# A factorisation-machine tower on one core: first tile gathered in two passes of 64 samples, the second pass transposed inside the first tile's steps

## The reference

```python
e = jnp.stack([tbl_0[ids[:, 0]], ..., tbl_32[ids[:, 32]]], axis=1)        # (1024, 33, 128)
row, col = np.triu_indices(33, k=1)
inner = x[:, row] * x[:, col]                                            # (1024, 528, 128)
fm = relu(einsum('bpd,ad->bpa', inner, attn_W) + attn_b)
scores = einsum('ba,bpa->bp', gnn_feature, fm)
attn = softmax(scores, axis=1)
attn_output = einsum('bp,bpd->bd', attn, inner) * 100.0
h = concatenate([gnn_feature, attn_output, gnn_feature], axis=1)
h = relu(h @ W_top1 + b_top1); h = relu(h @ W_top2 + b_top2); y = h @ W_top3
```

## Time and profile before

| what | value |
|---|---|
| median of 3 runs | 1306.75 us |
| the profiled execution, its own time | 1305.15 us |
| its span, first to last instruction | 1303.1 us |
| granted TensorE clock, mean | 1.000 |
| TensorE busy | 1219.5 us (94%) |
| VectorE busy | 1160.7 us (89%) |
| ScalarE busy | 1066.3 us (82%) |
| GpSimd busy | 479.5 us (37%) |
| DMA, mean over the span | 45 GB/s |

### The profile page before, as it was taken

The page is one execution under the profiler, slowest core; times in us unless marked ns, Lnnn a source line. Parts: engine busy times, 40 slices in busy tenths (PEclk is TensorE's granted clock), DMA queues, the critical chain, the costliest instruction groups (busy, mean ns, idle before and its releaser), DMA issues.

```text
span 1303.1 us, 22956 instructions
## 1 busy us (share of the span) xinstructions
PE 1219.5 (94%) x9486; PEld 951.5 (73%) x9486; DVE 1160.7 (89%) x643; ACT 1066.3 (82%) x1166; POOL 479.5 (37%) x271
## 2 busy tenths in 40 slices
PE   1499999999999999999999999999999999999997
PEld 1377777777777877778777777777777787777776
DVE  2499899997999989998999989999899988999964
ACT  2488999789887998879987799878988799877872
POOL 6586784018800486006840088102880000000000
DMA  3212310311113111130102111031111300012000
GB/s 105 99 34 85 64 30 25 108 37 29 33 27 109 31 28 27 29 114 25 32 24 86 58 31 31 15 112 38 29 31 29 104 17 1 1 44 59 13 1 1
DMA packets 54294, 58.58 MB, mean 45 GB/s; under 512 B 10536, under 2 KB 48560, under 8 KB 53168
## 3 DMA queue, kind: packets, MB, share of 16 engines
q1 hardware_dynamic: 45728, 39.81, 10.2%
q0 software_dynamic: 8448, 17.32, 5.0%
q10 hardware_dynamic: 16, 0.00, 0.0%
HBM read 36.12 MB, written 17.31 MB: 41 GB/s over the span
## 4 chain that ended last, share of the span: by engine, by line
PE 69%; ACT 18%; issue 9%; POOL 2%; DVE 1%; DMA 0%; ACTq 0%; POOLq 0%
PE scores L551 19%; PE ring L522 13%; PE ring L529 11%; PE ring L531 9%; PE ring L530 9%; ACT inner_hi L284 8%; ACT fm L276 8%; PE ring L579 4%; POOL x_rows L252 2%; PE ring L561 2%; PE ring L596 1%; PE scores L607 1%; ACT exp_pairs L292 1%; ACT attn L300 1%; DVE inner L391 1%
## 5 line engine op out<-in xcount | busy, mean ns | idle before, releaser
L276 ACT ACTIVATE fm<-ring,attn_b_sb 128x704 f32<-128x704 f32 x768 | 621.8, 867 | 165.6 <-PE ring L522 95.5
L391 DVE TENSOR_TENSOR inner<-xt 128x2112 f32<-128x2112 f32 x256 | 602.3, 2353 | 90.0 <-PE ring L531 37.8
L252 POOL DMA_INDIRECT x_rows<-in_tbl,ids_all x264 | 477.0, 1807 | 496.6 <-PE ring L561 407.0
L398 DVE TENSOR_TENSOR inner_lo<-inner,inner_hi 128x1760 fp32r<-128x1760 f32 (+2 forms) x256 | 473.5, 1850 | 18.1 <-ACT inner_hi L284 17.9
L529 PE MATMUL ring<-inner_hi,attn_wt_lo 128*128 128x352 f32 x1185 | 452.4, 382 | 20.3 <-ACT fm L276 17.3
L284 ACT CAST inner_hi<-inner 128x1760 fp32r<-128x1760 f32 (+2 forms) x256 | 401.0, 1567 | 5.4 <-DVE inner L391 5.4
L530 PE MATMUL ring<-inner_lo,attn_wt_hi 128*128 128x352 f32 x1185 | 382.4, 323 | 0.0
L531 PE MATMUL ring<-inner_hi,attn_wt_hi 128*128 128x352 f32 x1185 | 382.2, 323 | 0.0
L529 PEld LDWEIGHTS ring<-inner_hi,attn_wt_lo 128*128 128x128 f32 x1185 | 222.8, 188 | 79.6 <-ACT fm L276 54.8
L522 PE MATMUL ring<-inner,attn_wt 128*128 128x352 f32 x702 | 265.8, 482 | 12.5 <-ACT fm L276 8.0
L551 PE MATMUL scores<-fm,gnn_blocks 128*32 128x264 f32 x4096 | 254.4, 389 | 3.9 <-ACT exp_pairs L292 3.0
(11 more groups left out here) (50 smaller groups left out, 268.5 us busy)
## 6 DMA issues: line engine op xcount, KB each, us to landing
x_dram<-x_rows SPq DMA_DIRECT2D x8, 2112.0 KB, 6.7
x_fields<-x_dram SPq DMA_DIRECT2D x120, 128.0 KB, 3.0
x_rows<-in_tbl,ids_all POOLq DMA_INDIRECT x264, 3.5
attn_t<-attn_turned SPq DMA_DIRECT2D x112, 32.0 KB, 1.9
w_sb<-in_W_top SPq DMA_DIRECT2D x2, 512.0 KB, 6.3
x_rows<-x_dram SPq DMA_DIRECT2D x8, 128.0 KB, 3.9
x_fields<-in_r_gnn_feature SPq DMA_DIRECT2D x1, 512.0 KB, 4.1
h<-in_W_top SPq DMA_DIRECT2D x1, 256.0 KB, 6.2
```

The source lines that it names most:

```text
L252: nc.gpsimd.indirect_dma_start(out=x_rows[:, f, :], out_offset=None, in_=tables[f], in_offset=bass.IndirectOffsetOnAxis(ap=ids_all[:, t, f ...
L276: nc.scalar.activation(dst, slot(("hidden", S, j))[:, :, 0:CHUNK], ACT.Relu, bias=attn_b_sb[:, 0:1]).then_inc(s_fm, 1)
L391: nc.vector.tensor_tensor(dst, a, b, ALU.mult).then_inc(s_inner, 1)
L398: nc.vector.tensor_tensor(inner_lo[:, S % LO_BUFS, 0:n * CHUNK], inner[:, S % INNER_BUFS, NATIVE[S] * CHUNK:], inner_hi[:, S % HI_BUFS, 0: ...
```

## The change

Tile 0 alone is gathered in two passes. The first 33 indirect DMAs fetch samples 0 to 63 (`EARLY`), the next 33 samples 64 to 127, with indices of their own, `ids_late`, which a second small DMA loads into partitions 0 to 63. TensorE transposes the early rows ahead of step 0 (64 columns instead of 128), ScalarE copies half as much. The late rows are transposed behind steps 8, 9, 10, 11 and 11 (`LATE_AT`), all 128 rows of a field by 128, of which ScalarE copies the upper 64 samples. The product of step 16 (sample 64) waits for them. Tile 1's gathers now wait for the late chunks and for the store of tile 0, which waits for both passes. The steps of the transposes of tile 1 (`XT_AT`) and all later tiles are as before.

```diff
+    EARLY = P // 2
+    LATE_AT = (8, 9, 10, 11, 11)
...
-        jobs = []
+        jobs = [("late", 0, c) for c in range(XJ) if t == 0 and s == LATE_AT[c]]
...
-    units = [("x_t", 0, c) for c in range(XJ)]
+    units = [("early", 0, c) for c in range(XJ)]
...
+        def xt_jobs(kind, t):
+            return {"early": 0, "late": XJ}.get(kind, XJ * (t + 1))
...
             def store_rows(t):
                 for c in range(XJ):
+                    if t == 0:
+                        sp.wait_ge(s_early[c], 16 * fields_in(c))
                     sp.wait_ge(s_gather[c], 16 * fields_in(c) * (t + 1))
...
             sp.dma_start(ids_all[:], ids.rearrange("(t p) f -> p t f", p=P)).then_inc(s_ids, 16)
+            sp.dma_start(ids_late[:], ids[EARLY:P, :]).then_inc(s_ids, 16)
...
                     if t > 0:
-                        pool.wait_ge(s_xt_done, XJ * (t - 1) + c + 1)
+                        pool.wait_ge(s_xt_done, XJ * t + c + 1)
                         pool.wait_ge(s_store, 16 * t)
...
-            pool.wait_ge(s_ids, 16)
-            for t in range(T):
+            pool.wait_ge(s_ids, 32)
+            for f in range(F):
+                nc.gpsimd.indirect_dma_start(
+                    out=x_rows[0:EARLY, f, :], out_offset=None, in_=tables[f],
+                    in_offset=bass.IndirectOffsetOnAxis(ap=ids_all[0:EARLY, 0, f:f + 1], axis=0),
+                ).then_inc(s_early[f // FU], 16)
+            for f in range(F):
+                nc.gpsimd.indirect_dma_start(
+                    out=x_rows[EARLY:P, f, :], out_offset=None, in_=tables[f],
+                    in_offset=bass.IndirectOffsetOnAxis(ap=ids_late[:, f:f + 1], axis=0),
+                ).then_inc(s_gather[f // FU], 16)
+            for t in range(1, T):
                 gather(t)
...
+                own = samples_of(kind)
+                src = slot((kind, t, c))[:, 0:h, 0:min(n, 4) * P].rearrange("p h (f b) -> p (h f) b", b=P)[:, :, own]
+                dst = xt[:, t % 2, own, FU * c:FU * c + n].rearrange("d b f -> d f b")
...
+                    if GROUPS * (S + 3) == EARLY:
+                        dve.wait_ge(s_xt_out, 2 * XJ)
+                        dve.wait_ge(s_repeat, 2 * (K // FU))
...
+            def transpose_x(kind, t, c):
+                signal, loads = (s_early[c], 1) if kind == "early" else (s_gather[c], t + 1)
+                pe.wait_ge(signal, 16 * fields_in(c) * loads)
...
+                rows = EARLY if kind == "early" else P
                 for n in range(fields_in(c)):
-                    last = nc.tensor.transpose(to[:, n // 4, n % 4 * P:(n % 4 + 1) * P], x_rows[:, FU * c + n, :], ident[:])
+                    last = nc.tensor.transpose(to[:, n // 4, n % 4 * P:n % 4 * P + rows], x_rows[0:rows, FU * c + n, :],
+                                               ident[0:rows, 0:rows])
```

More of the change, by code:

```diff
@@ L82, in afm_tower @@
         ids_all = sb("ids_all", [P, T, F], I32)
+        ids_late = sb("ids_late", [P - EARLY, F], I32)
         x_rows = sb("x_rows", [P, F, D])
@@ L131, in afm_tower @@
         s_gather = [sem(f"rows_gathered{c}") for c in range(XJ)]
+        s_early = [sem(f"early_rows_gathered{c}") for c in range(XJ)]
         s_store = sem("rows_stored")
@@ L177, in taken_out, with samples_of @@
                 return s_mlp_out, 3 * a + b + 1
-            return s_xt_out, XJ * a + b + 1
+            return s_xt_out, xt_jobs(kind, a) + b + 1
+        def xt_jobs(kind, t):
+            return {"early": 0, "late": XJ}.get(kind, XJ * (t + 1))
+        def samples_of(kind):
+            return {"early": slice(0, EARLY), "late": slice(EARLY, P)}.get(kind, slice(0, P))
         def fields_in(c):
@@ L300, in scale_attn, with repeat, evacuate_xt @@
                 nc.scalar.activation(attn[:], src, ACT.Copy, scale=inv_sum[:, 0:1]).then_inc(s_attn, 1)
-            def repeat(t, c):
-                act.wait_ge(s_xt_out, XJ * t + c + 1)
-                x = xt[:, t % 2]
+            def repeat(kind, t, c):
+                act.wait_ge(s_xt_out, xt_jobs(kind, t) + c + 1)
+                x = xt[:, t % 2, samples_of(kind)]
                 nc.scalar.copy(x[:, :, F + FU * c:F + FU * c + FU], x[:, :, FU * c:FU * c + FU]).then_inc(s_repeat, 1)
-            def evacuate_xt(t, c):
-                act.wait_ge(s_xt_done, XJ * t + c + 1)
+            def evacuate_xt(kind, t, c):
+                act.wait_ge(s_xt_done, xt_jobs(kind, t) + c + 1)
                 if t > 1:
@@ L337, in _ @@
             for c in range(XJ):
-                evacuate_xt(0, c)
+                evacuate_xt("early", 0, c)
                 if c < K // FU:
-                    repeat(0, c)
+                    repeat("early", 0, c)
             round_inner(0)
@@ L354, in _ @@
                 for kind, of, c in jobs_of(S):
-                    if kind == "x_t":
-                        evacuate_xt(of, c)
+                    if kind in ("x_t", "late"):
+                        evacuate_xt(kind, of, c)
+                    if kind == "late" and c < K // FU:
+                        repeat(kind, of, c)
                     if kind == "mlp":
@@ L359, in _ @@
                 if t + 1 < T and s - 1 in XT_AT[0:K // FU]:
-                    repeat(t + 1, XT_AT.index(s - 1))
+                    repeat("x_t", t + 1, XT_AT.index(s - 1))
             exps(T - 1)
@@ L617, in _ @@
             for c in range(XJ):
-                transpose_x(0, c)
+                transpose_x("early", 0, c)
             pe.wait_ge(s_zero, 3)
@@ L624, in _ @@
                         fields(of, c)
-                    if kind == "x_t":
-                        transpose_x(of, c)
+                    if kind in ("x_t", "late"):
+                        transpose_x(kind, of, c)
                     if kind == "mlp":
```

14 lines of the change are left out of this document (5 added, 9 removed).

## The result

| | median, us | runs |
|---|---|---|
| before | 1306.45 | 4 (1304.79 to 1306.79) |
| after | 1325.20 | 4 (1323.39 to 1328.22) |

The ratio is 1.015 (95% interval 1.0138 to 1.0163): the change makes the kernel 18.8 us slower. The forecast was 1318 us, 11 to 12 us slower, with a range of 1304 to 1330. The profiled execution after took 1325.23 us, its span is 1323.5 us (before 1303.1), its mean granted clock 0.992.

The account below looks back on a forecast made before the run. The pitch of GpSimd's gathers was taken to set the first 50 us, TensorE, VectorE and ScalarE being near-equally busy after. Terms -8.7 + 4.5 + 4.5 + 11 + 1 = +12.3 gave about 1319, stated as 1318 us, range 1304 to 1330.

Parts of the forecast that it names:

- rival A: The forecast itself: slower by 12 us (6 to 18 over g of 0.55 to 0.8); chance 0.60.
- g: Time in us of one 64-row gather on GpSimd: taken as 0.70, between 0.47 and 0.94.
- rival B: A gather of 64 rows costs what one of 128 does: +22 us, 1329; chance 0.15.
- The start: Before the first product: smaller early gathers, transposes and copies gain 8.7 us (1.0 to 16.1).
- One gather per VectorE instruction: Beside the steps GpSimd does one gather per VectorE instruction, two per step, whatever a gather costs by itself.
- Rival C: Late pass not held to one gather per VectorE instruction, 1.0 us a gather: faster, 1302.5 us; chance 0.12.
- Late transposes and copies: Steps 8 to 11 of tile 0: 33 more transposes and copies in halves cost 4.5 us (2.8 to 5.6).
- Step 11: TensorE idles 5.8 us for late chunk 3; with extra gathers in VectorE's gaps, cost 4.5 us (1 to 7).
- Tile 1: Its gathers start at 119.0, behind late pass and store; TensorE waits sum to 12.9, cost 11 us (7 to 14).
- The clock: Slow TensorE weight loads after the longer waits: 0 to 2.5 us for each of two, 1 us in all.

Follow-up runs that it names:

- e3: Kernel before, with 30 measuring gathers of 16 to 128 rows ahead of tile 0's, VectorE idle or beside its products and reductions: 1363.97 us.
- e7: Changed kernel with the products of steps 2 to 27 of tile 0 each in two instructions of 1056 elements: 1307.33 us, ratio 1.001.
- e9: Kernel before with the products of steps 2 to 27 of tile 0 each in two instructions of 1056 elements: 1309.05 us, ratio 1.0003.
- e1: Changed kernel with tile 1's transposes behind steps 19, 22, 26, 28 and 28 of tile 0: 1348.71 us, with the stop of ScalarE at the start.
- e2: Changed kernel, but tile 0 gathered in one pass of 128 rows, transposes and copies still in halves: 1311.96 us, ratio 1.0025 to the kernel before.
- e5: The changed kernel once more, word for word, on another group's chip: 1325.34 us, ratio 1.0144 to the kernel before.
- e8: Changed kernel with 12 and 16 useless TensorE matmuls in the waits of 6.09 and 7.60 us: 1327.17 us, ratio 1.0159 to the kernel before.
- e12: Changed kernel, tile 1's transposes at steps 20, 23, 26, 28, 28 and 12 useless matmuls in step 11; same kernel as e10, another chip: 1319.99 us.
- e10: Changed kernel, tile 1's transposes at steps 20, 23, 26, 28, 28 and 12 useless matmuls in step 11: 1352.33 us, with the stop of ScalarE.
- e11: e7 with tile 1's chunks 3 and 4 transposed one step later each (steps 18, 20, 22, 25, 27): 1350.82 us, with the stop of ScalarE.

## Why the prediction was right, and what was mis-sized

The direction, the place and the mechanism were right. The size was not: the loss is 18.8 us, and rival A, the forecast, had 6 to 18 with g between 0.55 and 0.8. Measured are g = 0.90 and 1325.2, which lies nearer to rival B's 1329 than to 1318. The time stands in the range because that was wide enough to hold most of B. The 7 us between forecast and median (8.1 between the forecast's sum of 12.3 and the 20.4 of the profiled spans) come from the start, and from the clock, whose error is partly hidden by one of the other sign in tile 1's waits.

- **The start: forecast -8.7, measured -3.0 to -3.2.** The mis-sized term is g, "I take the middle, 0.70". It is 0.90 in the changed kernel, 0.91 in e3, near the upper bound of 0.94. The formula held within 0.9 us: 19.4 + 32 x 0.90 = 48.2, measured 47.30. This is 5.5 to 5.7 us of the miss. Rival B had this cost nearly right, and by its sentence (the Trainium skill, page "DMA: Bandwidth & Descriptors", section "Anatomy of one DMA — SWDGE (gpsimd) path": many descriptors can be emitted before their number is felt) the runs agree: in e3 128 rows cost 0.09 us more than 16. Its total of 1329 overshot by 4 us: it gave the start a gain of 1.0 us, where there were 3.0, while its costs of 23.5 us in sum agree with the 23.4 of the rows; the rest is that the medians differ by 18.8 us and the profiled spans by 20.4.
- **One gather per VectorE instruction: right**, with two amendments. e3 has it at 2.26 us a gather beside two-input products and no hold-up beside one-input reductions; e7 turns it into time, 18 us for a third instruction end per step, with e9 as control. And e9 shows that an end is worth a gather only if the gather is ready for it: 128 rows miss the third end that 64 rows catch. Rival C is refuted (the late gathers come at 1.98 us, not 1.0), and with it, for indirect DMAs, the inference in the Trainium skill, page "SBUF — State Buffer", section "Who interferes with whom", that the preparation of DMAs isn't held up.
- **Late transposes and copies: forecast 4.5, measured 5.0** up to the reduction of step 12, in e1 and in e2 alike (5.6 and 5.2 up to the end), inside the bounds of 2.8 to 5.6.
- **Step 11: computed 5.8, taken 4.5, a wait of 6.09 measured.** It cost 7.3 us beyond the late work, of which some 3 are the clock. The further gathers in VectorE's gaps, for which I took 1.3 us off, did not shorten it.
- **Tile 1: forecast 11, measured 10.5, and that agreement is luck.** The 10.5 hold 2.7 us of slow clock, which had a term of its own. The waits themselves were forecast at 12.9 us and are 9.07: 3.3, 5.8 and 3.8 forecast, 1.47, 7.60 and none measured (1.39 for the fourth in e5). The first gather was forecast at 119.0 and came at 119.48. The slow TensorE behind step 11 and each wait let gathers slip in, which I had counted only inside the waits.
- **The clock: forecast 1 in all, 5 to 6 in the rows.** Behind step 11 the transposes and the first matmuls were 3 us slower (e8), and in step 22 the transposes and the reduction took 0.9 and 1.8 us more. That is some 3 us behind the wait of step 11 and 2.7 behind that of step 22, both above the 2.5 us that the prediction gave as the most for one. But this isn't what the kernel would win back: with the clock held up in step 11 (e8, e12) the end came no sooner, as GpSimd's gathers set the next wait, in both runs behind a store that was 2.2 us slower. As a term of a sum it overlaps with the waits.

The sum with the measured values, from the reductions: late work 5.0, step 11 beyond it 7.3 (a pair of 18.02 us against 10.71 in e1), tile 1 10.5, up to the end 0.6, less 3.0 at the start: 20.4, the difference of the spans. It has to come out, since the ruler only divides the span; what it shows is how the 20.4 us divide.

## What to carry to other kernels

An indirect DMA on GpSimd is paid by the instruction and hardly by the row (0.94 us for 128 rows, 0.85 for 16): a pipeline that should start sooner needs fewer gathers ahead of its first work, not smaller ones. Where GpSimd gathers beside a busy VectorE, count the ends of VectorE's two-input instructions; that count is the most gathers that can get through, and fewer do where two ends are nearer than a gather's own time (1.20 us with 64 rows, 1.25 with 128). What is added in front of a queue must be paid by whatever stands behind it, here the next tile, whose gathers begin at 119.48 instead of 54.85. Before a wait is shortened, ask which engine sets the next one: time saved ahead of a queue that is counted in instructions comes back as a longer wait.

## What the runs showed that I had not expected

**A stop of ScalarE on two of the chips.** The kernel of e10 and e12 is one and the same. ScalarE's copies of the early rows (line L342) in e10:

```profile
26.99 1.06 ACT L342 COPY xt<-ring 128x512 f32<-128x512 f32 x1 [7.80 <-issue]
...
41.08 1.06 ACT L342 COPY xt<-ring 128x512 f32<-128x512 f32 x1 [12.34 <-remote]
63.48 1.07 ACT L342 COPY xt<-ring 128x512 f32<-128x512 f32 x1 [21.34 <-remote]
```

and in e12:

```profile
36.37 1.07 ACT L342 COPY xt<-ring 128x512 f32<-128x512 f32 x1 [7.83 <-PE ring L598]
46.11 1.18 ACT L342 COPY xt<-ring 128x512 f32<-128x512 f32 x2 [8.68 <-PE ring L598]
```

TensorE's transposes for the copies at 41.08 and 63.48 in e10 were these:

```profile
35.40 1.11 PE L598 MATMUL ring<-ident,x_rows 64*128 64x64 f32 x8 [8.45 <-DMA x_rows<-in_tbl,ids_all]
45.13 1.08 PE L598 MATMUL ring<-ident,x_rows 64*128 64x64 f32 x8 [8.62 <-DMA x_rows<-in_tbl,ids_all]
```

The first ended at 36.5, the second at 46.2; ScalarE started the copies 4.6 and 17.3 us later. From copy to copy it is 22.40 us in e1, e10 and e11 alike. The first product comes at 66.58 instead of 47.33, and some 20 us more are lost before the reduction of step 2 (103.43 instead of 63.44). In every execution of these kernels there the time was so (1351.63 to 1352.90 in e10). The runs with the stop were on two chips on which the kernel before takes 1308.8 and 1309.1 us; without it, on chips where it takes 1305.7 to 1306.5. The single-pass kernels lose about 2.5 us there: in e9 the last copy starts at 50.74 behind 9.96 us of "remote", where before it started at 48.27. The same kernel took 1352.33 us on a chip of the first kind and 1319.99 us on one of the second, and none of the four kernels with two passes that ran on such chips was free of the stop. Two passes may thus cost far more than 19 us there. The changed kernel itself was not run on such a chip, and each chip was used in one group of runs, so chip and occasion are not told apart. Whether it is the signal from TensorE or ScalarE itself that is late, and why while GpSimd gathers, no view shows; that stays open.

**The clock after a wait.** In the changed kernel, by stretch, around the end of the wait of 6.09 us and behind that of 1.47 us:

```profile
115.00:116.00 1.00, 1.00 (x4) 0.75 (x3) 0.17 (x1) 0.24 (x1) 0.00 (x0) 0.50 1.27 541
116.00:117.00 1.00, 1.00 (x8) 1.00 (x7) 1.00 (x1) 1.00 (x2) 0.00 (x0) 0.92 0.91 389
...
154.40:158.00 3.60, 3.60 (x43) 2.26 (x43) 1.99 (x1) 3.60 (x4) 2.99 (x3) 1.00 0.09 23
```

From 111.20 to about 116.1 TensorE works at 1.2 GHz, some 5 us; behind the short wait it never leaves 2.4 GHz. At the start of the program the recorded level is no guide: there the nine transposes of before take the same slow 2.18 us with a granted clock of 1.00 in 46.00:50.50, as did the slow weight loads that the prediction read. Why the record says so is open.
